# Choosing and scattering the experts' rows inside the attention before them, with GpSimd

## What is computed

```python
scores = xf @ router_w.T                      # 8 experts
top_v, top_i = jax.lax.top_k(scores, 2)
routing_w = jax.nn.softmax(top_v, axis=-1)
for e in range(8):
    w_e = jnp.sum(jnp.where(top_i == e, routing_w, 0.0), axis=-1)
    h = jax.nn.gelu(xf @ expert_w1[e].T, approximate=False)
    out = out + h @ expert_w2[e].T * w_e[:, None]
```

## Time and profile before

| | |
|---|---|
| Median of 3 runs | 5323.51 us (5317.22 to 5327.42) |
| Profiled execution | 5320.46 us |
| Its span | 5318.7 us |
| PE / PEld busy | 4172.8 / 2106.4 us |
| DVE busy | 3541.8 us |
| ACT busy | 2850.0 us |
| POOL busy | 1612.8 us |
| Granted TensorE clock, mean | 0.914 |

### The profile page before, as it was taken

One profiled execution on the slowest core, in us unless ns is written; L12 is line 12 of the kernel. 1 busy time (PEld: TensorE's weight loads), 2 busy tenths in 40 slices (PEclk: granted clock), 3 DMA queues, 4 the chain that ended last, 5 costly groups with the idle time before them and its releaser, 6 DMA issues. The chain is left out here.

```text
span 5318.7 us, 109649 instructions
## 1 busy us (share of the span) xinstructions
PE 4172.8 (78%) x31637; PEld 2106.4 (40%) x31638; DVE 3541.8 (67%) x8801; ACT 2850.0 (54%) x5331; POOL 1612.8 (30%) x1559
## 2 busy tenths in 40 slices
PE   6499999898667677778789999933987699983598
PEld 3144444552222222226222222323983244442497
DVE  3388888647899998984499999831116788873012
ACT  7255555676555555556667777721325466662232
POOL 3000000011777777741200000055536000006552
PEclk9699999999899998999889999966999799995799
DMA  7522222106100010000722222213665333321466
GB/s 257 150 73 72 74 76 72 33 0 216 42 26 26 26 36 28 26 13 2 244 73 74 78 76 75 72 38 123 214 189 209 108 95 96 98 77 46 142 212 191
DMA packets 546193, 502.03 MB, mean 94 GB/s; under 512 B 163774, under 2 KB 482911, under 8 KB 545788
## 3 DMA queue, kind: packets, MB, share of 16 engines
q1 hardware_dynamic: 527724, 460.95, 29.2%
q0 software_dynamic: 18160, 37.42, 2.1%
HBM read 330.57 MB, written 167.58 MB: 94 GB/s over the span
## 5 line engine op out<-in xcount | busy, mean ns | idle before, releaser
L1428 ACT ACTIVATE p_probs<-p_t_ps 128x512 f32<-128x512 f32 (+1 forms) x2304 | 1141.8, 551 | 680.9 <-PE p_t_ps L1320 243.8
L1963 PE MATMUL p_y_ps<-p_prod,c_ident 128*128 128x512 f32 x1024 | 554.5, 667 | 295.5 <-DVE p_prod L2148 290.9
L1333 PE MATMUL p_o_ps<-p_probs,p_v_st 128*32 128x256 f32 (+3 forms) x8704 | 727.0, 407 | 3.2 <-ACT p_o_sb L1414 2.9
L1465 DVE TENSOR_REDUCE p_row_max<-p_s_ps 128x1 f32<-128x512 f32 x1072 | 669.0, 680 | 71.9 <-PE p_s_ps L1271 55.6
L1254 POOL TENSOR_TENSOR p_v_st<-p_v_raw,p_ones 128x128 f32<-128x128 f32 x192 | 87.5, 456 | 2068.4 <-PE p_o_ps L1333 1946.9
L2097 POOL TENSOR_TENSOR p_dbx<-p_dtx,p_b_sb 128x512 f32<-128x512 f32 x512 | 632.4, 1267 | 113.2 <-ACT p_b_sb L1994 112.4
L2139 DVE TENSOR_TENSOR_SCAN p_state<-p_da,p_dbx 128x512 f32<-128x512 f32 x512 | 598.8, 1208 | 84.6 <-ACT p_da L2032 67.0
L1302 PE MATMUL p_t_ps<-p_t_q,p_t_k 50*128 50x512 bf16 (+3 forms) x3072 | 516.4, 336 | 147.6 <-ACT p_probs L1428 58.6
L1271 PE MATMUL p_s_ps<-p_s_k,p_s_q 48*128 48x512 bf16 (+3 forms) x3216 | 508.6, 340 | 146.8 <-DMA p_s_k<-stack_k 75.0
L1462 DVE CUSTOM_DVE_ANT_0 p_tried<-p_s_ps,p_s_bias 128x512 bf16<-128x512 f32 (+3 forms) x1072 | 470.5, 485 | 137.0 <-PE p_s_ps L1271 134.4
L1462 DVE CUSTOM_DVE_ANT_0 p_tried<-p_s_ps,c_mask_row 128x512 bf16<-128x512 f32 (+3 forms) x1072 | 470.5, 485 | 86.2 <-PE p_s_ps L1271 76.2
(11 more groups left out here) (256 smaller groups left out, 6888.0 us busy)
## 6 DMA issues: line engine op xcount, KB each, us to landing
p_wb<-in_w SPq DMA_DIRECT2D x142, 512.0 KB
p_s_q<-stack_q SPq DMA_DIRECT2D x408, 96.0 KB
p_s_k<-stack_k SPq DMA_DIRECT2D x408, 96.0 KB
p_t_q<-stack_q SPq DMA_DIRECT2D x390, 96.0 KB
p_t_k<-stack_k SPq DMA_DIRECT2D x390, 96.0 KB
mamba_inputs<-p_out SPq DMA_DIRECT2D x17, 1536.0 KB, 5.7
p_inp<-mamba_inputs SPq DMA_DIRECT2D x17, 1536.0 KB
stack_q<-p_parts SPq DMA_DIRECT2D x51, 384.0 KB
```

Source lines behind the costliest of these rows:

```text
L1333: mm = pe.matmul(o_ps[32 * j:32 * j + 32, at:to], v_st[:, g % 2, c, j, :], probs[:, g % 2, j, place[c] + at - first:place[c] + to - first] ...
L1428: act.activation(exps, tile, ACT.Exp, scale=scale).then_inc(expd, 1)
L1465: read = dve.tensor_reduce(found, scores, X, ALU.max)
L1963: pe.matmul(y_ps[:, h], w["ident"], prod[:, k_slot(n, h, RS)], start=(n == 0), stop=(n == STATE - 1)).then_inc(acc_mm, 1)
```

## The change

`route_tokens` is gone as a stage. A class `Routing` does its work inside `attend` of the latent and of the rotary attention, on single batches (`QT` is 4 token tiles, not 16). While the attention works on batch b, POOL copies batch b - 1 of the finished `x` (`stage_x`); PE turns it and multiplies by the router in one matmul of 136 columns a token tile, in two halves which are further uses of the `misc` bank (RA in the fourth group, RB in the first group of the next batch); ACT copies the halves out, sums squares and takes the deviation; POOL chooses (`choose`, batch b - 2, in the second group), scales the rows and parts (third group), ACT takes the exponentials and logarithms of the weights, PE counts with RA, and POOL places the rows (`locate`, batch b - 3, in the first group) and scatters them, four in the first group and four in the third. POOL's stream over the 16 batches is unrolled. The last two batches are chosen, scaled and placed by DVE after the attention's last add; POOL scatters the last three there, DVE works out the plan and SP fills the tails with the same instructions as before. Tables are loaded at the attention's start, the zeros for spares are written there by POOL, and SP fills the spares after batch 1, in the latent attention only. `run_tiles` and `add_back` are unchanged; the plan lies in a slice of `xn`.

Further, in all three attentions: scores, maxima, shifts and loads of groups past the last are no longer made (`exists`), `project` no longer stores a batch past the end, and batch 15 stands unrolled behind the loop. A routed causal attention's loop starts at batch 2; the latent attention's loop makes four turns of three batches instead of five.

```diff
+QT = T // P
+WIDE = P + E
+RING_ROWS = 2
...
+    def turned(self, pe, misc, half):
+        for j in range(2):
+            c = 2 * half + j
+            mm = pe.matmul(misc[:, WIDE * j:WIDE * j + WIDE], self.staged_x[:, c * P:(c + 1) * P], self.turn_w[:, :],
+                           start=True, stop=True)
...
+    def choose(self, eng, then, m):
+        eng.wait_ge(self.rstd_ready, m + 1)
+        if m >= 1:
+            eng.wait_ge(self.counted, m)
+        shape = [P, QT, E, E]
+        then(eng.tensor_tensor(self.logits[:, :, :], self.raw[:, :, P:WIDE],
+                               self.rstd[:, :].unsqueeze(2).to_broadcast([P, QT, E]), ALU.mult))
+        then(eng.tensor_tensor(self.differ[:, :, :, :], self.logits[:, :, :].unsqueeze(2).to_broadcast(shape),
+                               self.logits[:, :, :].unsqueeze(3).to_broadcast(shape), ALU.subtract))
+        then(eng.tensor_scalar(self.ahead[:, :, :, :], self.differ[:, :, :, :], 0.0, None, ALU.is_gt))
+        then(eng.tensor_scalar(self.differ[:, :, :, :], self.differ[:, :, :, :], 0.0, None, ALU.is_equal))
+        then(eng.tensor_tensor(self.differ[:, :, :, :], self.differ[:, :, :, :],
+                               self.tables["earlier"].unsqueeze(1).to_broadcast(shape), ALU.mult))
+        then(eng.tensor_tensor(self.ahead[:, :, :, :], self.ahead[:, :, :, :], self.differ[:, :, :, :], ALU.add))
+        then(eng.tensor_tensor(self.half[:, :, :, :], self.ahead[:, :, :, 0:4], self.ahead[:, :, :, 4:8], ALU.add))
+        then(eng.tensor_tensor(self.pairs[:, :, :, :], self.half[:, :, :, 0:2], self.half[:, :, :, 2:4], ALU.add))
+        then(eng.tensor_tensor(self.rank[:, :, :], self.pairs[:, :, :, 0], self.pairs[:, :, :, 1], ALU.add))
+        for r in range(TOPK):
+            then(eng.tensor_scalar(self.is_rank[:, r], self.rank[:, :, :], float(r), None, ALU.is_equal))
+        eng.tensor_tensor(self.chosen[:, :, :], self.is_rank[:, 0], self.is_rank[:, 1], ALU.add
+                          ).then_inc(self.chosen_ready, 1)
+        both = [P, TOPK, QT, E]
+        then(eng.tensor_tensor(self.masked[:, :, :, :], self.is_rank[:, :, :, :],
+                               self.logits[:, :, :].unsqueeze(1).to_broadcast(both), ALU.mult))
+        self.folded(eng, then, self.best)
+        if m >= 1:
+            eng.wait_ge(self.parts_ready, m)
+        eng.tensor_tensor(self.behind[:, :], self.best[:, 1], self.best[:, 0], ALU.subtract).then_inc(self.lead_ready, 1)
+    def folded(self, eng, then, out):
+        then(eng.tensor_tensor(self.masked4[:, :, :, :], self.masked[:, :, :, 0:4], self.masked[:, :, :, 4:8], ALU.add))
+        then(eng.tensor_tensor(self.masked2[:, :, :, :], self.masked4[:, :, :, 0:2], self.masked4[:, :, :, 2:4], ALU.add))
+        then(eng.tensor_tensor(out[:, :, :], self.masked2[:, :, :, 0], self.masked2[:, :, :, 1], ALU.add))
+    def scale_rows(self, eng, then, m):
+        u = m % RING_ROWS
+        if m >= RING_ROWS:
+            eng.wait_ge(self.sent[u], 16 * TOPK * QT * (m // RING_ROWS))
+        by = self.rstd[:, :].unsqueeze(2).to_broadcast([P, QT, P])
+        for r in range(TOPK):
+            eng.tensor_tensor(self.rows[:, u, r, :, 0:P], self.raw[:, :, 0:P], by, ALU.mult).then_inc(self.raw_read, 1)
+        eng.tensor_copy(self.rows[:, u, :, :, P + 1].bitcast(I32), self.tables["home"][:, :, QT * m:QT * m + QT]
+                        ).then_inc(self.rows_ready, 1)
+    def parts(self, eng, m):
+        eng.wait_ge(self.log_ready, 2 * m + 2)
+        eng.wait_ge(self.lead_ready, m + 1)
+        eng.tensor_tensor(self.part_log[:, 1], self.behind[:, :], self.norm_log[:, :], ALU.subtract)
+        eng.tensor_scalar(self.part_log[:, 0], self.norm_log[:, :], -1.0, None, ALU.mult).then_inc(self.parts_ready, 1)
+    def locate(self, eng, then, m):
+        u = m % RING_ROWS
+        eng.wait_ge(self.counted, m + 1)
+        now, following = self.base[:, m % 2], self.base[:, 1 - m % 2]
+        for t in range(QT):
+            then(eng.tensor_tensor(now[:, t + 1], now[:, t], self.counts[:, 1, t], ALU.add))
+        eng.tensor_copy(following[:, 0], now[:, QT])
+        then(eng.tensor_tensor(self.place[:, :, :], self.counts[:, 0], now[:, 0:QT], ALU.add))
+        both = [P, TOPK, QT, E]
+        then(eng.tensor_tensor(self.masked[:, :, :, :], self.is_rank[:, :, :, :],
+                               self.place[:, :, :].unsqueeze(1).to_broadcast(both), ALU.mult))
+        self.folded(eng, then, self.slot)
+        eng.tensor_copy(self.index[:, u], self.slot[:, :, :]).then_inc(self.located, 1)
+        eng.wait_ge(self.part_ready, m + 1)
+        eng.wait_ge(self.rows_ready, m + 1)
+        eng.tensor_copy(self.rows[:, u, :, :, P], self.part[:, :, :]).then_inc(self.marked, 1)
+    def scatter(self, pool, m, at, to):
+        u = m % RING_ROWS
+        if at == 0:
+            pool.wait_ge(self.raw_read, TOPK * m + TOPK)
+            pool.wait_ge(self.located, m + 1)
+            pool.wait_ge(self.marked, m + 1)
+        for k in range(at, to):
+            r, t = k // QT, k % QT
+            pool.indirect_dma_start(self.rows_dram, bass.IndirectOffsetOnAxis(self.index[:, u, r, t:t + 1], 0),
+                                    self.rows[:, u, r, t, :], None).then_inc(self.sent[u], 16)
...
+    def empty_rows(self, pool):
+        pool.wait_ge(self.loaded, 16 * len(self.loads))
+        pool.tensor_copy(self.base[:, 0, 0], self.tables["region"]).then_inc(self.begun, 1)
+        if self.empty_now:
+            pool.memset(self.nothing, 0.0).then_inc(self.emptied, 1)
+            pool.wait_ge(self.emptied, 1)
+            pool.tensor_copy(self.nothing[:, :, :, P + 1].bitcast(I32), self.tables["nowhere"]).then_inc(self.emptied, 1)
+        pool.wait_ge(self.begun, 1)
+    def fill_tails(self, sp):
+        sp.wait_ge(self.tail_ready, 1)
+        for e in range(E):
+            at = sp.value_load(self.tail[0:1, e:e + 1], min_val=e * REGION, max_val=e * REGION + NTOK)
+            sp.dma_start(self.rows_dram[ds(at, R)].rearrange("(p c) f -> p c f", c=C), self.nothing[:, e]
+                         ).then_inc(self.filled, 16)
+        sp.wait_ge(self.filled, 16 * (E + SPARE if self.empty_now else E))
...
+    FROM, TO = (2 if UNROLL == 1 and routed else UNROLL), NB - 1
+    GROUPS = 4 * NB
...
+        def exists(b, k):
+            return not isinstance(b, int) or 4 * b + k < GROUPS
...
-            store(NB, (NB - 1) % PB)
...
+            def stage_x(m, added, read):
+                pool.wait_ge(misc_read, added + 1)
+                if read is not None:
+                    pool.wait_ge(misc_mm, read + 1)
+                pool.tensor_copy(rt.staged_x[:, :], x[:, T * m:T * m + T]).then_inc(rt.x_staged, 1)
+            rt.empty_rows(pool)
+            for b in range(NB):
+                values(b, 0)
+                if b >= 3:
+                    rt.locate(pool, then, b - 3)
+                    rt.scatter(pool, b - 3, 0, 4)
+                values(b, 1)
+                if b >= 2:
+                    rt.choose(pool, then, b - 2)
+                values(b, 2)
+                if b >= 2:
+                    rt.scale_rows(pool, then, b - 2)
+                    rt.parts(pool, b - 2)
+                if b >= 3:
+                    rt.scatter(pool, b - 3, 4, 8)
+                values(b, 3)
+                if b >= 1:
+                    stage_x(b - 1, use_no(b, 2, "WO"), use_no(b, 0, "RB") if b >= 2 else None)
+            rt.locate(pool, then, NB - 3)
+            pool.sem_inc(rt.begun, 1)
+            rt.scatter(pool, NB - 3, 0, 8)
+            stage_x(NB - 1, end_use("WO"), end_use("RB"))
+            rt.scatter(pool, NB - 2, 0, 8)
+            rt.scatter(pool, NB - 1, 0, 8)
+            for u in range(RING_ROWS):
+                pool.wait_ge(rt.sent[u], 16 * TOPK * QT * (NB // RING_ROWS))
...
+                    if rt and at == misc_at["RB"] and g == 0 and started >= 8:
+                        routed_half(use_no(b, g, "RB"), b - 2, 1).then_inc(misc_mm, 1)
+                    if rt and at == misc_at["RA"] and g == 3 and started >= 4:
+                        mm = routed_half(use_no(b, g, "RA"), b - 1, 0)
+                        if started >= 8:
+                            mm = rt.count(pe, misc, b - 2)
+                        mm.then_inc(misc_mm, 1)
...
+            def deviation(no, m):
+                act.wait_ge(misc_read, no + 1)
+                for t in range(QT):
+                    act.activation(rt.square[:, t], rt.raw[:, t, 0:P], ACT.Square, accum_out=rt.sums[:, t:t + 1]
+                                   ).then_inc(rt.squared, 1)
+                act.wait_ge(rt.squared, (QT + 1) * m + QT)
+                act.activation(rt.sums[:, :], rt.sums[:, :], ACT.Ln, bias=rt.norm_w["eps"], scale=1.0 / P
+                               ).then_inc(rt.squared, 1)
+                act.wait_ge(rt.squared, (QT + 1) * m + QT + 1)
```

(31 more changed lines are left out.)

559 lines of the change are left out of this document (259 added, 300 removed).

## The result

The changed kernel takes 5251.17 us (median of 4 runs, 5248.06 to 5253.41) against 5320.36 us for the kernel before (5317.08 to 5327.42): ratio 0.9868, 95% interval 0.9854 to 0.9883. It takes 69 us less (1.3%), where 234 less were forecast. The profiled execution has a span of 5251.6 us, against 5318.7. This is not the result on every chip: on four others the kernel before took 5270 to 5277 us, and on one of these the changed kernel's profiled execution took 5057.9. A second execution there took 7104.7 us at a mean granted clock of 0.646; it has no profile, is not explained, and is left out of what follows.

A forecast was written before the change was run, and what follows sets the result against it. No engine was full: PE and DVE were busiest in the attentions, POOL's scatters filled most of the routing stages. 5320.5 - 270.9 - 16 - 15 - 7 + 72 + 3 gave 5086.6, as median 5090 us; range 4952 to 5130.

The forecast's parts named there:

- Added inside the attentions: Extra PE and ACT work in both routed attentions: 2.6 and 2.2 us a batch, 72 us in all.
- The removed stages: Both routing stages between an attention's last add and the tiles' first matmul go: 228.9 + 227.0 us.
- the store past the end: The extra store of a batch in three projections, 5.3 us each, goes: 16 us saved.
- The tail: Work left after each attention's last add: 92.5 us with SP at its slow pace, 41 at its usual pace.
- Rival A: SP fills the tails at its usual pace after the last add: 4987 us; chance 0.36.
- I cost it at nothing: POOL's routing work inside the attentions, 27 us a batch, fits within the batch and adds 0 us.
- My own sign of being wrong: Inside the attentions, DVE or SP waiting for POOL, or small steps of 0.70 us, would show the forecast wrong.
- Rival B: POOL or ACT late inside the attentions, up to 4 us a batch: + 75, 5165 us; chance 0.07.
- C: POOL becomes the attentions' bound from 50 us a batch, slower than before: 5410 at 53 us; chance 0.05.
- One loop turn less: The first of the two attentions' loop goes 4 times, not 5; one jump less saves 7 us.
- The Trainium skill's rule: Elementwise work belongs on VectorE; in the attentions, POOL's arithmetic there was estimated at 8 us a batch, 240 us.
- Rival D: The second attention's loop no longer stays loaded, stalling at each of 13 jumps: + 90, 5180 us; chance 0.02.

The follow-up runs named there:

- late_scatter: The changed kernel with the 104 scatters of batches 0 to 12 moved behind each attention, on a chip with stalls: 5347.6 us.
- alone_again: scatter_alone to the letter, run again on a third chip, without stalls: 5274.2 us, with the kernel before at 5272.0.
- scatter_alone: The kernel before plus eight scatters of zeros a batch, in two bursts of four inside both routed attentions, on a chip with stalls: 5513.3 us.

## Why the prediction was wrong, step by step

Against the 5086.6 us forecast for the profiled execution, 5253.4 is 167 us more. The stalls are 187 of them, the other additions inside the two attentions 71 (see *Added inside the attentions*), the tails 105 the other way, and the remaining 14 lie in small pieces. That the result is only 167 us off is partly luck: a gain that I did not take hides half of a loss that I did not see.

- *The removed stages* and *the store past the end* were right: 228.9 and 227.0 us are gone, and the first attention with its projection gave 7.1 us, of which 5.3 are the store by its price. That leaves 1.8 us for its scores past the end, where I took 5; my least was 0. In the two others the last batch, where such a saving would show, did not get shorter: on a chip without stalls 25.8 us instead of 22.8, and 24.1 instead of 16.8.
- *The tail.* The step that takes 92.5 us because SP goes at 0.70 us an instruction is wrong, and the figure beside it, 41 us, was right: 39.9 both times. Rival A was true, 105 us more gain than the forecast. SP's pace is not a property of its instructions. In `late_scatter`, where 104 more scatters follow in the same tail, the same eight tails took 22.8 us in the first tail and 35.3 in the second:

```profile
L587 SPq DMA_DIRECT2D routed_rows<-xn x8: 3/698/715, 4849.8 to 4885.1; - x8
```

  And on a chip without stalls (the first routing stage of `alone_again`, unchanged from the kernel before) they took 7.8 under the full 128 scatters:

```profile
L467 SPq DMA_DIRECT2D routed_rows<-xn x8: 332/332/358, 3533.3 to 3541.1; - x8
```

  Slow SP steps and stopped engines were seen together and were gone together. I had named "only 8 scatters instead of a flood of 128" as the reason for A, and that fits these runs.
- *POOL, "I cost it at nothing".* This is the step that failed. The prices held: 318 us busy in 790, 21 us a batch and the gaps besides, against my 27, and POOL waited 148 us for PE. What I did not ask is what an indirect DMA does to the other engines. On this chip eight scatters cost 5.7 to 8.7 us a batch, in which PE, DVE and ACT stop together: 187 us, of which part is PE's work at half clock behind the stops. My own sign of being wrong came true, the small steps of 0.70 us inside the attentions. The row that should have warned me is the earlier trace rows itself: I read SP's 0.70 us steps as something of that stage, priced them only there, and moved the scatters beside four working engines at nothing. Rival B had a loss inside the attentions, but by POOL being late, and 75 us; C had POOL as the bound, by a scatter that costs POOL more beside working engines (0.99 us each, 0.97 before). Neither mechanism happened.
- *Added inside the attentions.* Without the scatters' stalls a batch costs 3.0 us more in the latent attention and 4.7 in the rotary one (`late_scatter`), against 2.6 and 2.2. From first add to last the changed kernel without stalls takes 55.3 us more in the latent attention (735.5 - 680.2) and 71.1 more in the rotary one (592.5 - 521.4), 126 in all, where my terms for these two stretches come to 55 (72, less 7 for the loop turn and 10 for the scores past the end): this term was mis-sized by 71 us. Of the 4.7 us, 2.4 are the squares, which agrees with the mechanism, PE and ACT waiting for each other behind lumps; the other 2.3 were not taken apart. I had given the rotary attention less because ACT has more idle time there. That its groups are shorter, so that the same lumps weigh more, may be why it was too little; no run shows it. What I left out is the clock: 1.00 there before, 0.95 with the additions.
- *One loop turn less.* Three long batches remain in `late_scatter`'s latent attention (54.8, 55.6 and 57.3 us against 48.1), where before there were four (52.6, 51.2, 52.6 and 51.2 against 45.0). One jump is gone, but the others cost 6.7 to 9.2 us instead of 6.2 to 7.6: 23.4 us in all instead of 27.6, so at most 4 of the 7 us were saved.
- *The Trainium skill's rule* that elementwise work belongs on VectorE ("GPSIMD Engine Reference", Engine selection): its factor holds for 512 elements (1.27 us against 0.68), and no run here moves the arithmetic to DVE, so what its conclusion would have cost stays my estimate. POOL's arithmetic is not in the 187 us, which come without any of it in `scatter_alone`. The Trainium skill's page "SBUF — State Buffer", Who interferes with whom, says that a DMA never contends with a compute engine, and that one that seems stalled by VectorE waits for GpSimd to write its descriptors. The chips without stalls agree (`alone_again`, 2 us); on the other, `scatter_alone` (188 us) shows the reverse of that exception, GpSimd's indirect DMAs stopping PE, DVE and ACT, so there the measurement decides.
- *Rival D* did not come either: the rotary loop's batches are even at 40.7 on the chips without stalls; no jump back shows in them.
- *The range* was not what its own bounds give: -42 and +48 us would make 4945 to 5138, and I wrote 4952 to 5130. The measured time lies outside both.

With the tails at 41 us my sum was 4987 (rival A), 336 us less than before. The chip without stalls gave 5058 against a kernel before of 5272: -214, of which -328 are the two tails (add to matmul 203 and 205 us in `alone_again`, to 40) and +114 the rest, against my +37 (-16 - 15 - 7 + 72 + 3).

## What to carry to other kernels

When work is moved under other work, price what its instructions do to the neighbours, DMAs above all, and not only its engine's time: look in the trace for any engine that went slowly while that instruction was running, even where it was hidden. Spread indirect DMAs from GpSimd between other work instead of issuing them in bursts: in pairs, half of the loss came back on the chip with stalls, and singly they cost nothing clear of the noise on chips without (5050 to 5076 us, 5057.9 with the bursts). Single ones where they stall, and pairs where they don't, were not measured. Run an experiment and its baseline on the same chip, and repeat the decisive one on another.

## What the runs showed of the hardware

- On one chip, and on the one of the result, indirect DMAs from GpSimd (128 rows of 520 bytes each) make the other engines start late on what they wait for, and PE, DVE and ACT stand idle together. A burst of four costs 2.8 to 4.4 us, a pair 0.5 to 1.4, and the stop begins 2 to 3.5 us after the first scatter; plain DMAs of the same rows, through the same queue, cost hardly anything. SP's small steps come 0.70 us apart in the same microseconds. On four other chips nothing of it shows, and the kernel before is 43 to 55 us faster there: its stages from add to matmul take 203 and 205 us (`alone_again`) instead of 229 and 227. What in the chip does it, and what makes the difference, stays open, and so does whether single scatters are free where fours are not: pairs are the smallest measured there.
- In the rotary attention of `scatter_alone` PE stops 26 times for 2.0 to 3.1 us, and 25 times its granted clock then falls to 0.50 (1.2 GHz) for a while (from 4380.5 in the slices above), 106 us in all. In `alone_again`, without the stops, it stays at 1.00, and PE's busy time is 47 us less. So a stop costs more than its length.
- An operation of 256 elements with one tensor input and a scalar takes longer on GpSimd, 0.87 us, than one with two tensor inputs, 0.61 to 0.73. On DVE in the tail the same two take 0.29 and 0.42 to 0.62 us.
